# Attention scores of a float32 transformer block: from one float32 product of 32-row tiles to two products of stacked hi and lo parts in the rounded format

## What is computed

```
q, k, v = split(x @ w_qkv.T);  k_y = x @ w_ky.T          (each split into heads)
agg = sum_k(exp(clip(q k_y^T / 4, -15, 15)) * tril) + eps
w   = softplus(log(|q k^T / 4| + eps) - log(agg + eps)) * tril
out = (w / (sum_k w + eps)) v @ w_proj.T
x   = layernorm(x + out)
h   = silu(x @ w1 * s1) * (x @ w2 * s2);  h = gelu(h @ h1 * ..);  h = gelu(h @ h2 * ..)
x   = layernorm(x + h @ w3 * s3)
```

## Time and profile before

| | us |
|---|---|
| median of 3 runs | 1370.33 (1370.06 to 1373.92) |
| the profiled execution | 1369.58 |
| its span, first to last instruction | 1367.8 |

### The profile page before, as it was taken

The page is one execution under the profiler, slowest core; times in us unless marked ns, Lnnn a source line. Parts: engine busy times, 40 slices in busy tenths (PEclk is TensorE's granted clock), DMA queues, the critical chain, the costliest instruction groups (busy, mean ns, idle before and its releaser), DMA issues.

```text
span 1367.8 us, 22887 instructions
## 1 busy us (share of the span) xinstructions
PE 1248.2 (91%) x8214; PEld 807.9 (59%) x8214; DVE 728.6 (53%) x1232; ACT 622.8 (46%) x819; POOL 138.2 (10%) x188
## 2 busy tenths in 40 slices
PE   4888999999999999875499999999999999999996
PEld 2433444444443444433388788787887878878785
DVE  2556778686877767675343534435244352443523
ACT  3666767767677766563232313223132231322311
POOL 1212122222221122220000000000000000000000
PEclk9999999999999999998799999999999999999998
DMA  2011312222321411000640000000000000000000
GB/s 90 1 55 32 97 60 96 73 92 77 101 83 46 138 46 55 1 31 32 230 180 16 31 0 16 31 15 31 0 15 31 15 31 0 15 31 15 31 0 16
DMA packets 31942, 66.88 MB, mean 49 GB/s; under 512 B 2848, under 2 KB 8608, under 8 KB 31904
## 3 DMA queue, kind: packets, MB, share of 16 engines
q1 hardware_dynamic: 31904, 66.35, 14.3%
HBM read 46.42 MB, written 19.92 MB: 49 GB/s over the span
## 4 chain that ended last, share of the span: by engine, by line
issue 51%; POOL 0%; DVE 0%; POOLq 0%; DVEq 0%
POOL f_rstd L865 0%; DVE f_res L872 0%; POOLq L965 0%; DVEq L877 0%; POOL f_minus_half L963 0%; POOLq L83 0%
## 5 line engine op out<-in xcount | busy, mean ns | idle before, releaser
L991 ACT ACTIVATE f_h_full<-f_layer_bank,f_scales 128x512 f32<-128x512 f32 x128 | 88.0, 687 | 354.7 <-PE f_layer_bank L1105 354.6
L380 ACT ACTIVATE e_ring<-score_banks 128x1024 f32<-128x1024 f32 (+1 forms) x192 | 158.8, 879 | 134.4 <-PE score_banks L704 134.2
L541 DVE TENSOR_TENSOR w_ring<-score_banks,keep 128x1024 int32<-128x1024 int32 (+1 forms) x192 | 191.8, 1041 | 48.5 <-PE score_banks L704 47.1
L1105 PE MATMUL f_layer_bank<-f_ha_hi,f_w_all 128*128 128x512 f32 x512 | 204.4, 399 | 2.8 <-DVE f_h_full L1033 2.3
L1105 PE MATMUL f_layer_bank<-f_hb_hi,f_w_all 128*128 128x512 f32 x512 | 202.6, 396 | 0.0
L1105 PE MATMUL f_layer_bank<-f_ha_lo,f_w_all 128*128 128x512 f32 x512 | 202.5, 396 | 0.0
L1105 PE MATMUL f_layer_bank<-f_hb_lo,f_w_all 128*128 128x512 f32 x512 | 202.4, 395 | 0.0
L532 DVE TENSOR_SCALAR e_ring<-e_ring 128x2048 f32<-128x2048 f32 (+1 forms) x96 | 100.4, 1046 | 114.3 <-ACT e_ring L380 114.2
L387 ACT ACTIVATE w_ring<-w_ring 128x2048 f32<-128x2048 f32 (+1 forms) x96 | 157.2, 1637 | 6.4 <-DVE w_ring L541 6.2
L293 POOL TENSOR_SCALAR_AFFINE_SELECT e_ring<-e_ring 128x512 f32<-128x512 f32 (+1 forms) x96 | 79.3, 826 | 438.1 <-DVE e_ring L532 437.3
L1105 PEld LDWEIGHTS f_layer_bank<-f_ha_hi,f_w_all 128*128 128x128 f32 x512 | 96.1, 188 | 33.9 <-DVE f_ha_lo L1025 6.5
(11 more groups left out here) (111 smaller groups left out, 1573.5 us busy)
## 6 DMA issues: line engine op xcount, KB each, us to landing
piece<-in_wf SPq DMA_DIRECT2D x44, 256.0 KB, 2.8
wf_copy<-piece SPq DMA_DIRECT2D x44, 256.0 KB, 2.9
f_w_all<-wf_copy SPq DMA_DIRECT2D x2, 4096.0 KB, 25.1
f_x_turn<-x SPq DMA_DIRECT2D x9, 512.0 KB, 3.3
xq<-in_xt SPq DMA_DIRECT2D x8, 512.0 KB, 4.5
xv<-in_xt SPq DMA_DIRECT2D x8, 512.0 KB, 3.8
res<-in_xn SPq DMA_DIRECT2D x8, 512.0 KB, 4.4
x<-res SPq DMA_DIRECT2D x8, 512.0 KB, 2.8
```

The source lines that it names most:

```text
L380: nc.scalar.activation(e_ring[:, t % RING, 2 * i:2 * i + 2, 0:cols], pair_banks(y_pair(t, i), cols), ACT.Exp).then_inc(exp_done, 1)
L541: nc.vector.tensor_tensor(w_ring[:, t % RING, 2 * i:2 * i + 2, 0:cols].bitcast(I32), pair_banks(w_pair(t, i), cols).bitcast(I32), keep[:, ...
L991: nc.scalar.activation(h_full[m % 2][:], f_bank[m % RING][:], ACT.Gelu, scale=scales[:, 1 + layer, m:m + 1]).then_inc(gelu_done, 1)
L1105: mm = nc.tensor.matmul(out, left.bitcast(dt), right.bitcast(dt), start=first and n == 0, stop=last and n == 1)
```

## The change

- `project` results are no longer masked into q[0] and q[1]. Each of q, ky, k, qc is kept in full, then split: hi (rounded to float32r) and lo (the rest, a subtraction). q: ScalarE copy and hi, VectorE lo. ky and k: ScalarE copy and hi, GpSimd lo. qc: all three on VectorE.
- DMAs on SyncE's queue stack the parts: in `q_stack[g]` and `qc_stack[g]` a head's hi rows lie on even and its lo rows on odd partitions; `ky_stack[g]` and `k_stack[g]` have two orders, hi/lo and lo/hi. With 16 channels and two parts a head fills 32 partitions.
- Each score product becomes two, orders 0 and 1, accumulated in PSUM, in float32r: (hi, lo) with (hi, lo), then (lo, hi) with (hi, lo). The four row tiles stay; the loop runs over the order outside and the tile inside.
- Quad g now is the four heads on partitions 64 g to 64 g + 63 (`(g r)` in place of `(r g)` in `of_quad`, `keep_att` and the stationary of `sum_weights`); the layout of the projections stays.
- `q_proj` moves from late beat 4 to beat 3 and `k_proj` from beat 3 to late beat 4, with their readers; the xq load moves to the even slot before.
- SyncE's slot gets `stack_qc`, `stack_ky`, `stack_q`, `stack_k` at written-out places, and `stack_q` and `stack_ky` of unit 0 stand ahead of the first slot; `make_quads` goes.

The diff, cut to its core (declarations and matching edits of strides left out; `stack_k` is written as `stack_ky` and `stack_qc` as `stack_q`, with `w_scores`; VectorE calls `q_rest` in beat 4 ahead of `clip`):

```diff
@@ SyncE
+            def stack(to, place, src, g, stacked):
+                there, here = to[place:P:2, :], src[64 * g:64 * g + 64, :]
+                sp.dma_start(there.bitcast(F32), here.bitcast(F32)).then_inc(stacked, 16)
+            def stack_q(u):
+                reach_alone(sp, q_lo_made, u.index + 1, sp_passed)
+                reach_alone(sp, y_scores, BEATS * (u.index - 1), sp_passed)
+                for g in range(2):
+                    stack(q_stack[g][u.half][:], 0, q_hi, g, q_stacked[g])
+                    stack(q_stack[g][u.half][:], 1, q_lo, g, q_stacked[g])
+            def stack_ky(u):
+                reach_alone(sp, ky_lo_made, u.index + 1, sp_passed)
+                reach_alone(sp, y_scores, BEATS * (u.index - 1), sp_passed)
+                for g in range(2):
+                    for order in range(2):
+                        stack(ky_stack[g][u.half][:, order, :], order, ky_hi, g, ky_stacked[g])
+                        stack(ky_stack[g][u.half][:, order, :], 1 - order, ky_lo, g, ky_stacked[g])
...
@@ SyncE slot
                 if check and check != "last":
                     load_piece(k, 2, check)
+                if 3 in w:
+                    stack_qc(k.shift(-1))
+                if project:
+                    stack_ky(k.shift(1))
+                if check and check != "last":
                     load_piece(k, 3, check)
+                if project:
+                    stack_q(k.shift(1))
                 if norm is not None:
                     reach_alone(sp, ln_step, LN_STEPS * (norm + 1), sp_passed)
                     sp.dma_start(x1[norm], res[:]).then_inc(x1_stored, 16)
+                if y:
+                    stack_k(k)
@@ GpSimd
+            def ky_rest(u):
+                reach_alone(pool, ky_hi_made, u.index + 1, pool_passed)
+                nc.gpsimd.tensor_tensor(ky_lo[:], ky_full[:], ky_hi[:].bitcast(F32), ALU.subtract).then_inc(ky_lo_made, 1)
...
+                    if t == 1 and project:
+                        ky_rest(k.shift(1))
+                    if t == 4 and y:
+                        k_rest(k)
@@ ScalarE
             def q_keep(u):
-                reach(act, y_scores, BEATS * (u.index - 1))
-                reach(act, qc_made, 2 * (u.index - 1))
-                nc.scalar.mul(q[0][u.half][:], misc[:], in_quad[:, 0:1]).then_inc(q0_made, 1)
+                reach(act, qc_made, u.index - 1)
+                nc.scalar.mul(q_full[u.half][:], misc[:], HD ** -0.5).then_inc(q_made, 1)
+            def q_halve(u):
+                reach(act, q_made, u.index + 1)
+                for g in range(2):
+                    reach(act, q_stacked[g], 32 * u.index)
+                nc.scalar.copy(q_hi[:], q_full[u.half][:]).then_inc(q_hi_made, 1)
             def ky_keep(u):
-                nc.scalar.copy(ky[u.half][:], misc[:]).then_inc(ky_made, 1)
+                nc.scalar.copy(ky_full[:], misc[:]).then_inc(ky_made, 1)
+                for g in range(2):
+                    reach(act, ky_stacked[g], 64 * u.index)
+                reach(act, ky_made, u.index + 1)
+                nc.scalar.copy(ky_hi[:], ky_full[:]).then_inc(ky_hi_made, 1)
@@ VectorE
-            def q_keep(u):
-                nc.vector.tensor_scalar(q[1][u.half][:], misc[:], in_quad[:, 1:2], None, ALU.mult).then_inc(q1_made, 1)
+            def q_rest(u):
+                reach(dve, q_hi_made, u.index + 1)
+                nc.vector.tensor_tensor(q_lo[:], q_full[u.half][:], q_hi[:].bitcast(F32), ALU.subtract).then_inc(q_lo_made, 1)
             def qc_make(v):
+                nc.vector.tensor_tensor(qc_full[:], misc[:], q_full[v.half][:], ALU.mult).then_inc(qc_made, 1)
                 for g in range(2):
-                    nc.vector.tensor_tensor(qc[g][v.half][:], misc[:], q[g][v.half][:], ALU.mult).then_inc(qc_made, 1)
+                    reach(dve, qc_stacked[g], 32 * v.index)
+                reach(dve, qc_made, v.index + 1)
+                nc.vector.tensor_copy(qc_hi[:], qc_full[:]).then_inc(qc_hi_made, 1)
+                reach(dve, qc_hi_made, v.index + 1)
+                nc.vector.tensor_tensor(qc_lo[:], qc_full[:], qc_hi[:].bitcast(F32), ALU.subtract).then_inc(qc_lo_made, 1)
@@ TensorE
             def q_proj(u):
-                take_misc((q0_made, u.index + 1), (q1_made, u.index + 1))
+                take_misc((q_made, u.index + 1))
             def scores(t, pair, left, right):
                 for at, j in CHUNK_TILES[t % CHUNKS]:
-                    for r in range(QUAD):
-                        mm = nc.tensor.matmul(score[:, 2 * pair(t, r // 2) + r % 2, at:at + T - P * j],
-                                              left[lanes(r), P * j:P * j + P], right[lanes(r), P * j:T], start=True, stop=True)
+                    for order in range(2):
+                        for r in range(QUAD):
+                            mm = nc.tensor.matmul(score[:, 2 * pair(t, r // 2) + r % 2, at:at + T - P * j],
+                                                  left[lanes(r), order, P * j:P * j + P], right[lanes(r), P * j:T],
+                                                  start=order == 0, stop=order == 1)
             def scores_w(k, t, y):
-                reach(pe, k_made, u.index + 1)
-                reach(pe, qc_made, 2 * u.index + 2)
+                reach(pe, k_stacked[g], 64 * (u.index + 1))
+                reach(pe, qc_stacked[g], 32 * (u.index + 1))
```

More of the change, by code:

```diff
@@ L105, in attention_phase @@
         w_hi, w_lo = sb("w_hi", [P, DT, 2, D], F32R), sb("w_lo", [P, DT, 2, D], F32R)
[L106 to L109, removed]
+        q_full = [sb(f"q_full{t}", [P, T]) for t in range(2)]
+        ky_full, k_full, qc_full = sb("ky_full", [P, T]), sb("k_full", [P, T]), sb("qc_full", [P, T])
+        q_hi, q_lo = sb("q_hi", [P, T], F32R), sb("q_lo", [P, T], F32R)
+        ky_hi, ky_lo = sb("ky_hi", [P, T], F32R), sb("ky_lo", [P, T], F32R)
+        k_hi, k_lo = sb("k_hi", [P, T], F32R), sb("k_lo", [P, T], F32R)
+        qc_hi, qc_lo = sb("qc_hi", [P, T], F32R), sb("qc_lo", [P, T], F32R)
+        q_stack = [[sb(f"q_stack{g}_{t}", [P, T], F32R) for t in range(2)] for g in range(2)]
+        qc_stack = [[sb(f"qc_stack{g}_{t}", [P, T], F32R) for t in range(2)] for g in range(2)]
+        ky_stack = [[sb(f"ky_stack{g}_{t}", [P, 2, T], F32R) for t in range(2)] for g in range(2)]
+        k_stack = [[sb(f"k_stack{g}_{t}", [P, 2, T], F32R) for t in range(2)] for g in range(2)]
         v_before = sb("v_before", [P, TI - 1, HU, HD])
@@ L427, in keep_att @@
                 sums = misc[:].rearrange("p (i r c) -> p i r c", i=TI, c=SW)
-                heads = att_raw[:, :, HU * u.half:HU * u.half + HU, :].rearrange("p i (r g) c -> p i r g c", g=2)
-                nc.scalar.copy(heads[:, :, :, m // CHUNKS, :], sums[:, :, :, 0:HD + 1]).then_inc(att_kept, 1)
+                heads = att_raw[:, :, HU * u.half:HU * u.half + HU, :].rearrange("p i (g r) c -> p i g r c", g=2)
+                nc.scalar.copy(heads[:, :, m // CHUNKS, :, :], sums[:, :, :, 0:HD + 1]).then_inc(att_kept, 1)
             def piece_halve(k, s):
@@ L449, in slot @@
                         base_make(k.shift(-1))
-                    if t == 3 and y:
-                        k_keep(k)
+                    if t == 3 and project:
+                        q_keep(k.shift(1))
+                        q_halve(k.shift(1))
                     if t == 4 and 0 in w:
@@ L463, in slot @@
                         turn_keep(out, 1)
-                    if t == 4 and project:
-                        q_keep(k.shift(1))
+                    if t == 4 and y:
+                        k_keep(k)
                     if t < STEPS and check and (check != "first" or t > 0) and (check != "last" or t == 0):
@@ L619, in slot @@
                         keep_agg(k, 0)
+                    if t == 4 and project:
+                        q_rest(k.shift(1))
                     if y:
@@ L644, in _ @@
             split_weights()
-            make_quads()
-            q_keep(Unit(0, 0))
+            q_rest(Unit(0, 0))
             make_keep()
@@ L814, in slot @@
                         spread_c(k.shift(-1))
-                    if t == 3 and y:
-                        k_proj(k)
+                    if t == 3 and project:
+                        q_proj(k.shift(1))
                     if t == 4 and (y or 0 in w):
@@ L832, in slot @@
                         project_out(norm, 1)
-                    if t == 4 and project:
-                        q_proj(k.shift(1))
+                    if t == 4 and y:
+                        k_proj(k)
                     if t == 5 and out is not None:
```

94 lines of the change are left out of this document (56 added, 38 removed).

## The result

The changed kernel takes 1358.5 us (median of 20 runs, 1354.9 to 1370.7) against 1370.5 for the kernel before (20 runs, 1368.7 to 1373.9): ratio 0.992, 95% interval 0.9907 to 0.9934. It is faster by 12 us where 32 were forecast: the way was right and the time lies in the range, the size is a third of the forecast. Of the runs of the experiments one, of the kernel before with filler, took 1793 us at a mean clock of 0.65 and is left out.

What follows compares the result with a forecast made beforehand. Latency loops through TensorE, ScalarE and VectorE, not TensorE's load alone, were taken to pace the attention units. Units -41, w-only beats -3.5, late stacks +4, start +5, drain +3.3: -32 us from 1369.6, so 1338, range 1312 to 1368.

Steps and rivals of the forecast that it cites:

- rival E: Score products: rounded-format row tiles run one after another, +9 us a unit, about 1520 us; chance 0.05.
- The start: Before the first score product: cast, subtraction, stacking issues and landing add 6.0, less 1.0 for the clock: +5 us.
- The qc chain: From qc_make in beat 2 to beat 3's w product: 5.6 us, slack 0.4 to 1.0; 4 us charged over 14 units.
- rival B: Beat 3's w product in 15 units: qc stacks land late and block TensorE, 1388 us at 7 us landing; chance 0.11.
- Rival D: Score products: weight loads of the second to fourth rounds are not covered, 1.5 us a unit, 1362 us; chance 0.07.
- 41 + 3.5 = 44.5 us: Gain from shorter score products: 41 us in ten loop units and six others, 3.5 in nine w-only beats.
- the side work: Added casts, subtractions and stacks: charged 12.3 us, as 5 at the start, 4 for late stacks, 3.3 in the drain.
- with the clock at its upper level (1.00) throughout: Attention phase of the kernel before, 578.3 us: TensorE's clock read as at its upper level all the time.
- The ends: Start +5 us; drain +3.3 us for the last unit's qc chain, covered only by a w-only beat.
- six others: The six units besides the ten loop units: 2.7 us saved in each, 16 us in all.
- 512 columns take 0.34 + 0.23 = 0.57: Score product of 512 columns, two rounds of four overlapping row tiles: 0.57 us, saving 0.50.
- I cost it at 0: Three added ScalarE casts per unit (q_hi, ky_hi, k_hi), with waits 2.1 us: priced at 0, bounds 0 and 2.1.

Runs made afterwards that it cites:

- e1: Changed kernel with all side work kept, but each score product as one plain float32 product, cross terms left out: 1381.2 us, 1.0078 of the kernel before.
- e2: Changed kernel with only order 0 of each score product, in the rounded format, cross terms left out: 1353.0 us, ratio 0.9879.
- e3: Changed kernel plus products of zeros where TensorE waits before sum_weights (beat 3 of every unit, beats 0 and 5 of odd ones): 1354.2 us, ratio 0.9888.
- e7: Changed kernel with the subtraction that makes qc_lo moved from VectorE to GpSimd: 1358.9 us, ratio 0.9908.
- e9: Changed kernel with one ScalarE instruction moved, the cast q_hi of beat 3 behind the logarithm: 1354.3 us, ratio 0.9884.
- e12: Changed kernel with e3's zero products and the hi stacks of qc and ky issued early, q_hi cast left in place: 1353.3 us, ratio 0.9875.
- e5: Changed kernel with e3's filler, and filler also in the first units, before the first score product and in the drain: 1354.4 us, ratio 0.9877.
- e11: Changed kernel with e3's zero products, the q_hi cast behind the logarithm and the hi stacks issued early: 1350.1 us, ratio 0.9851.

## Why the prediction was right and wrong

**Right.** The reading of the bound: shorter products shorten the beats only by the loop's share. In units 4 to 14 TensorE's busy time fell by 29.7 us and their length by 14.9. The four row tiles overlap in the rounded format (rival E fell), and a further round costs 0.24 us. The odd unit, 36.0 us for 36.2, is right by luck in part: the product gave less than forecast, and it still came out shorter. The start: +4.6 for +5 (in e1, e2, e3, e7 and e9, which start alike, the first product stands at 26.1 to 27.4 us, +5 to +7), by another split: an issue takes SyncE 0.60 us where I took 0.5, landing 2.5 for 2.7. The qc chain: in units 4 to 14 of the changed kernel TensorE did not wait for a stack, so the 4 us charged there were not due, and rival B fell. It fell narrowly: the slack was counted as 0.4 to 1.0 us and is 0.1 to 0.6 us in even units. The load of the DMA engines was taken too low, about 50% where even units show 0.75. Rival D fell too, in the timeline of beat 3 of unit 12:

```profile
461.57 0.30 PEld L781 LDWEIGHTS score_banks<-q_stack,ky_stack 32*128 32x128 f32 x8 [1.31 <-DVE w_ring L614]
461.58 0.74 PE L781 MATMUL score_banks<-q_stack,ky_stack 32*128 32x512 f32 x8 [0.62 <-DVE w_ring L614]
```

All eight loads, those of the second round among them, are done after 0.30 us, before the second round's matmuls start (461.91), while the first round streams to the same row tiles. The Trainium skill, TensorE: Matmul & The Clock Gate, Part 3 (The mechanism), says that weight loads overlap running matmuls "only when row_grp differs"; the trace disagrees in the rounded format as well.

**Wrong.** The step that failed is the gain of the products in the sum, 41 + 3.5 = 44.5 us: it is 22.7 (e1 against the change, medians), while the side work was 10.9 for 12.3. The reasons, on the profiled execution (1363.7 against a sum of 1337 to 1338, 26 us; on the medians 20):

1. *"with the clock at its upper level (1.00) throughout"*: the sum took this as given after the change. It isn't. Shorter products make TensorE wait longer for ScalarE (1.07 to 1.45 us, 1.09 to 1.48), and behind most falls to 1.2 GHz stands an idle time of about 1.5 us. In units 4 to 14 that is 7.8 us (e3), shown on the profiled executions; 4.3 us on the medians. In the first units it is part of the miss too: e12, with 3.4 us at the lower clock in units 1 to 3 where the changed kernel has 13.7, takes 122.3 us in units 0 to 3 for 128.0. The filler and the earlier stacks of e12 have a part in this that no run separates. No rival of mine named the clock.
2. *The ends.* Units 0 to 3 were given 2.7 us each as "six others" and gained nothing, and the drain was given -2.9 and cost +4.7. In e1, the side work with the old product, they take 3.4 and 5.2 us more than before, part of it at the lower clock, while the steady units take no more than before: the ends have less cover for casts and stacks, and I priced only the last qc chain. Unit 0 did not shorten at all (24.5 us before and after); what paces its y-only beats was not tried, and 10.8 us of it ran at the lower clock. How the rest of the drain's loss is shared by clock and stacks stays open: e5 had 20 us less of the lower clock there and got 3.3 us back.
3. *"512 columns take 0.34 + 0.23 = 0.57"*, and likewise 0.63 and 0.35: 0.67, 0.78 and 0.44 measured. Streaming was right (e2), the edge of about 0.1 us per product was left out. The y side saves 1.8 us a unit, not 2.5, at most 0.7 x 16 = 11 us. Less than that came through: with the clock held, units 4 to 14 take 390.9 us (e3) for the 385.9 forecast without late stacks, so this and the next point have 5 us there together.
4. *"I cost it at 0"* for the casts on ScalarE: q_hi ahead of the logarithm costs an even unit 0.4 us (e9), and 3.2 us on the median (e11 against e12). The argument that the logarithm has room in beat 3 was false; besides, in even units it is the side work that makes most of the idle time (1.07 of 1.45 us).

These sizes overlap and are not to be added. What stands is 22.7 us of product gain less 10.9 of side work: 12. Holding the clock and moving the cast, with the early stacks (e11), gives 8 us of the missing 20 back; for the other 12, the products' edges and the ends are the known causes, and their shares stay open.

## What to carry to other kernels

An edit that makes the busiest engine less busy also lengthens its single idle times; look in the profile how long its longest ones are while its clock stands at the upper level, and price a fall as a case of its own. What is newly put ahead of the instruction that the busiest engine waits for (here a cast ahead of the logarithm) is not free because its own engine is half idle: order it behind. And fill and drain have no cover: price every added step there on its own, or measure the side work with the old product, as e1 does.

## What the runs showed of the hardware

- The granted clock fell to half in otherwise dense work for 3.4 us or more at a time. In units 0 to 14 of the changed kernel there are nine such falls, seven of them behind a single idle time of 1.4 to 1.5 us; where no idle time was longer than 1.2 us (units 4 to 14 before, in e3 and e11) it held for 389 to 414 us. It also held behind single idle times of 1.33 us (e1), 1.42 us (e5) and 1.53 us (unit 15 before).
- Products of zeros that do nothing else made the kernel 4 us faster (e3 against the change, 1354.2 for 1358.5); in the kernel before, where no clock was lost in the units that they fill, they were free (1.0005).
- One round of four row tiles in the rounded format, 32 rows x 512 columns each, takes 0.43 us alone and 0.24 us more for a second one on the same banks.
- A DMA inside SBUF of 64 rows x 2 KB to every other partition held SyncE for 0.60 us and landed 2.4 to 2.5 us after its issue; 24 of them a unit raised the DMA share from 0.29 to 0.75 in even units without TensorE waiting for one in units 4 to 14.
